# A gated linear-attention block: k's rope by plain transfers and one more VectorE operation

## The chip, the cores and the metric

The kernel is one launch on one core of one Trainium2 chip. The metric is the device time in microseconds (us). Everything is in float32; the large matrix products are made of three products of parts (high by high, low by high, high by low), which is why each weight and each activation exists as a `_hi` and a `_lo` tile.

## The reference, cut to what matters

The block takes x (2048 tokens of 512), normalises it, and computes an attention part and a feed-forward part that gates it. The attention part has 16 heads of 128 channels. For q and k of each head:

```python
q = causal_dwconv(silu(x @ Wq), conv_q_w)      # 4 taps; k and v alike
def rot_half(u):
    u1, u2 = jnp.split(u, 2, axis=-1)
    return jnp.concatenate([-u2, u1], axis=-1)
q = q * cos + rot_half(q) * sin
k = k * cos + rot_half(k) * sin
q = q / max(norm(q), 1e-12); k = k / max(norm(k), 1e-12)
for s in range(4):                             # the 4 lags
    attn = (q * lag(k, s)).sum(-1) / sqrt(128)
    out += attn * sigmoid(lag(a, s) * b) * lag(v, s)
out = out * rsqrt(mean(out * out) + eps) * norm_w * silu(x @ Wz)
s = out @ Wout
```

The result is x + s * silu(ffn(x)). The two lines of the rope are what the change is about. On the chip the 128 channels of a head lie on the 128 partitions, so rot_half moves data from partitions 0 to 63 to partitions 64 to 127 and back. [...]

## The kernel before, in words

The attention part is a software pipeline over 64 steps: head h = 0 to 15, and in each head four chunks g = 0 to 3 of 512 tokens. A step is counted c = 4h + g. Each of the five engines has a `step` function with its own order of the work, in which `c - 1`, `c - 2` and so on are chunks of earlier steps. There is no scheduler: the order is the order of the code, and the engines meet at counting semaphores.

- **TensorE** (`step`, L1070) projects q, k and v of chunk c (12 products each, L997), turns the squares for the norms (L1054), projects z of chunk c-2, computes the scores of chunk c-2 (L1066) and the sums over the values of chunk c-3 (L1042).
- **ScalarE** reads the projections out through silu (L662), makes the first tap of each convolution (L676) and the squares (L703, L704).
- **VectorE** (`step`, L880) does the other nine taps (`conv_tap`, L812), transposes v (`turn_v`, L852), does its part of the rope (`rope`, L831 and L835), reduces the norms (`sum_fold`, L842), multiplies the scores by the gates and by a band mask (`gate_scores` L858, `mask_band` L867), joins and scales the output (L818, `make_o` L875), and in g = 3 splits the next head's weights of q, k and v (`split_lo`, L823), in g = 1 those of z. TensorE's first product for a head's k waits for `wlo_k` (`wait(pe, wlo_done[n], h + 1)`, L994).
- **GpSimd (POOL)** (`step`, L577) starts the accumulating transfers (`fold_squares` L568, `add_swapped` L574, `add_squares` L562), takes the roots of the norms (`roots`, L528 and L532), and makes the gates (`make_gates`, L548 to L556).
- **SyncE (SP)** (`step`, L437) issues the plain transfers, in this order in a step: weights, `store_v` of c-1 (L416), `store_rq` of c (three small stores of the roots, L402 to L405), `load_rq` of c-2 (L412), `store_o` (L430), `load_v` of c-1 (four, L426). `load_rq` waits until the three stores have landed (L409), and `make_gates` for chunk c-2 waits for `load_rq` in the next step.

The rope of n in "qk" before: VectorE writes `rot = y * cos` (L831) and `swapped = y * sin` (L835, with the sign in the table), then POOL's `add_swapped` starts two transfers of 64 partitions each that add `swapped` to `rot` with the halves exchanged (L573 to L575). The scores wait for those transfers through `wait_rope` (L332, L1059 to L1062). For k, the two VectorE operations stand in the step after the one that made y_k: `rope("k", 0, ...)` after the first q tap and `rope("k", 1, ...)` after the second.

After the 64 steps the last chunks run out of the pipeline, and the feed-forward and the output product follow, which the change does not touch.

Of the kernel before, what the change touches and what calls it, by code (L numbers as in the profile page):

```python
# [205 lines left out]
def attention(nc, env):  # L206
# [20 lines left out]
    NC = H * G  # L227
    HALF = D // 2
# [69 lines left out]
    conv_done = {n: sem(f"conv_done_{n}") for n in "qkv"}  # L298
    rope_done = {n: sem(f"rope_done_{n}") for n in "qk"}
    rope_asked = sem("rope_asked")  # L300
    rope_added = {n: [sem(f"rope_added_{n}{i}") for i in range(2)] for n in "qk"}
    squares_done = sem("squares_done")
    fold_asked = sem("fold_asked")
    folded = sem("folded")
# [26 lines left out]

    def wait_rope(eng, n, g, c):  # L332

        wait(eng, rope_added[n][g % 2], 32 * (c // 2 + 1) if isinstance(c, int) else
             c * 16 + (32 if g % 2 == 0 else 16))

    def wait_v(eng, g, c):
# [30 lines left out]
    def cols(g):  # L368
        return slice(g * CH, (g + 1) * CH)

    def on_sync(sp):
# [65 lines left out]
        def step(h, g):  # L437
            c = h * G + g
            if not is_last(h):
                if g == 0:  # L440
                    for n in "qkv":
                        load_weights(n, h + 1)
                if g == 2:
                    load_weights("z", h + 1)
            if at := back(h, g, 1):
                store_v(at[1], c - 1)
                store_rq(at[1], c)
            if at := back(h, g, 2):
                load_rq(at[1], c)
            if at := back(h, g, 3):  # L450
                store_o(at[0], at[1], c - 3)
            if at := back(h, g, 1):
                load_v(at[1], c - 1)
# [20 lines left out]
    def on_gpsimd(pool):  # L474
# [102 lines left out]
        def step(h, g):  # L577
            c = h * G + g
            if at := back(h, g, 1):
                fold_squares(at[1], c)  # L580
                add_swapped("q", at[1], c - 1)
            if at := back(h, g, 3):
                make_gates(at[1], c - 3)
            if at := back(h, g, 1):
                add_swapped("k", at[1], c - 1)
            if at := back(h, g, 4):
                add_squares(at[1], c - 4)
            if at := back(h, g, 1):
                roots(at[0], at[1], c)
                if is_start(h, g - 1):  # L590
                    pool.wait_ge(gate_done, 2)
                gate_keys(at[0], at[1], c)

        schedule(pool, step)
        for n in "qk":
            add_swapped(n, G - 1, NC - 1)
        roots(H - 1, G - 1, NC)
        gate_keys(H - 1, G - 1, NC)
        make_gates(G - 3, NC - 3)
# [7 lines left out]
    def on_scalar(act):  # L607
# [51 lines left out]
        def silu_and_tap(n, bank, h, g, c):  # L659
            wait(act, proj_done[n], c + 1)  # L660
            wait(act, conv_done[n], DVE_TAPS[n] * (c - 1))
            nc.scalar.activation(u[n][:, g % 2, HALO:], bank[:, :], ACT.Silu).then_inc(silu_done[n], 1)  # L662

            wait(act, conv_done[n], DVE_TAPS[n] * c)
            wait(act, silu_done[n], 2 * c + 1)
            if n == "v":
                wait(act, v_stored, 16 * (c - 1))
            else:
                wait(act, rope_done[n], 2 * (c - 1))
            if g < G - 1:  # L670
                nc.scalar.activation(u[n][:, (g + 1) % 2, 0:HALO], bank[:, CH - HALO:CH], ACT.Silu
                                     ).then_inc(silu_done[n], 1)
            else:
                nc.scalar.activation(u[n][:, 0, 0:HALO], rot["q"][:, S:S + HALO], ACT.Copy
                                     ).then_inc(silu_done[n], 1)
            nc.scalar.activation(y[n][:, g % 2, :], u[n][:, g % 2, 0:CH], ACT.Copy,  # L676
                                 scale=cw[n][:, bass.ds(h * TAPS, 1)]).then_inc(tap_done[n], 1)
# [70 lines left out]
        square_out(NC - 4)  # L748
        silu_z(G - 2, NC - 2, bank_kz)
        for n in "qk":  # L750
            act.wait_ge(rope_done[n], 2 * NC)
            for i in range(2):
                act.wait_ge(rope_added[n][i], 16 * NC)
        ffn.hidden(0, 0)
        save_spill(G - 3, NC)
        silu_z(G - 1, NC - 1, bank_qv)
# [14 lines left out]
    def on_vector(dve):  # L771
# [53 lines left out]

        def rope(n, i, g, c):

            wait(dve, conv_done[n], 3 * c + 3)
            if i == 0:
                wait(dve, scores_done, c - 3)  # L830
                op = nc.vector.tensor_tensor(rot[n][:, cols(g)], y[n][:, g % 2, :], cos[:, cols(g)], ALU.mult)  # L831
            else:
                if not (isinstance(c, int) and c < 2):
                    wait_rope(dve, n, g, c - 2)
                op = nc.vector.tensor_tensor(swapped[n][:, g % 2, :], y[n][:, g % 2, :], sin[:, cols(g)],  # L835
                                             ALU.mult)
            op.then_inc(rope_done[n], 1)
# [42 lines left out]
        def step(h, g):  # L880
# [14 lines left out]
            if at3:  # L895
                gate_scores(at3[1], c - 3)
                mask_band(at3[1], c - 3)
            conv_tap("k", 3, h, g, c)
            if is_start(h, g):
                dve.wait_ge(ab_turned, 1)  # L900
# [47 lines left out]
        turn_v(G - 1, NC - 1)  # L948
        rope("k", 0, G - 1, NC - 1)
        rope("k", 1, G - 1, NC - 1)  # L950
        sum_fold(G - 1, NC)
        gate_scores(G - 3, NC - 3)
        mask_band(G - 3, NC - 3)
# [15 lines left out]
    def on_tensor(pe):  # L969
# [86 lines left out]

        def score(g2, k):
            ahead = 1 if g2 < G - 1 else 0
            wait_rope(pe, "k", g2, k)  # L1059
            wait_rope(pe, "q", g2, k)  # L1060
            if ahead:
                wait_rope(pe, "q", g2 + 1, k + 1)  # L1062
# [543 lines left out]
```

## Time and profile before

| | |
|---|---|
| median of 3 runs | 1326.75 us (1324.55 to 1327.91) |
| profiled execution | 1327.47 us, of which 1325.7 us span from the first to the last instruction |
| TensorE busy (matmul) | 1292.8 us, 98% of the span |
| VectorE busy | 954.7 us, 72% |
| ScalarE busy | 720.5 us, 54% |
| GpSimd busy | 641.8 us, 48% |
| attention steps, by the slices of the page | about 70 to 890 us |

The busy shares are means over stages with different limits: VectorE is at 9 tenths and more in the attention steps and at 2 to 4 tenths behind them. A matmul's end is modelled, so a TensorE that reads 98% may still have been held up by short waits; the rows below are read for those. The granted TensorE clock is at 9 tenths or more of full speed in all but one of the 40 slices of the page.

### The profile page before, as it was taken

How to read it: one execution, taken by the hardware profiler on the slowest of the kernel's cores; microseconds unless marked ns; L12 is line 12 of the kernel's file. 1: busy time of each engine (PE TensorE's matmuls, PEld its weight loads, DVE VectorE, ACT ScalarE, POOL GpSimd, SP SyncE). 2: the span in 40 equal slices, each digit the busy share in tenths (PEclk: the TensorE clock that was granted, in tenths of full speed). 3: DMA queues.
4: the chain of work that ended last, by engine and by line, in shares of the span. 5: the costliest groups of instructions: out<-in, count | busy, mean ns of one | idle time of the engine just before them, and what ended most of it. 6: DMA issues, size and time to landing. Idle time of an engine off the chain costs nothing.

```text
span 1325.7 us, 22085 instructions
## 1 busy us (share of the span) xinstructions
PE 1292.8 (98%) x6312; PEld 1078.7 (81%) x6312; DVE 954.7 (72%) x1530; ACT 720.5 (54%) x1377; POOL 641.8 (48%) x827
## 2 busy tenths in 40 slices
PE   6989999999999999999999999998999999999998
PEld 5778888888888888888888888877888888888886
DVE  7879999989999999899999998993122322423442
ACT  5656666666666666666666666664543444422221
POOL 6357676777776767767767777763000000000001
PEclk9989999999999999999999999999999999999999
DMA  8258888888797888787878787868510101246544
GB/s 267 63 108 174 157 157 157 169 149 171 139 177 149 163 155 166 153 170 142 174 153 162 150 164 154 153 121 221 178 47 18 47 16 56 85 154 213 184 124 138
DMA packets 276875, 188.89 MB, mean 142 GB/s; under 512 B 167904, under 2 KB 204768, under 8 KB 276576
## 3 DMA queue, kind: packets, MB, share of 16 engines
q1 hardware_dynamic: 238064, 121.48, 34.1%
q0 software_dynamic: 38768, 66.87, 31.1%
q8 instruction: 23, 0.38, 0.1%
q14 instruction: 20, 0.16, 0.1%
HBM read 79.36 MB, written 42.08 MB: 92 GB/s over the span
## 4 chain that ended last, share of the span: by engine, by line
PE 77%; DVE 11%; issue 5%; DMA 3%; POOL 2%; ACT 2%; SPq 1%; DVEq 0%; POOLq 0%; ACTq 0%
PE bank L997 37%; PE bank L1491 13%; PE bank L1294 9%; PE bank L1281 8%; PE bank L1066 3%; PE bank L1042 3%; DVE y_k L812 2%; DVE y_q L812 2%; PE bank L1054 2%; DVE y_v L812 2%; PE bank L987 1%; ACT y_q L676 1%; DMA rq_win<-rq_scratch 1%; DVE coef L858 1%; DVE rot_k L831 1%
## 5 line engine op out<-in xcount | busy, mean ns | idle before, releaser
L812 DVE SCALAR_TENSOR_TENSOR y_q<-u_q,cw_q,y_q 128x512 f32<-128x512 f32 x192 | 143.0, 745 | 57.7 <-ACT y_q L676 57.6
L1362 POOL TENSOR_TENSOR g_buf<-g_buf,up_raw 128x512 f32<-128x512 f32 x3 | 3.8, 1280 | 356.2 <-DVE g_buf L1422 356.2
L1270 DVE TENSOR_TENSOR hid_lo<-relu,hid_hi 128x512 fp32r<-128x512 f32 x64 | 44.3, 693 | 166.4 <-ACT hid_hi L1262 166.4
L812 DVE SCALAR_TENSOR_TENSOR y_k<-u_k,cw_k,y_k 128x512 f32<-128x512 f32 x192 | 143.4, 747 | 1.3 <-ACT y_k L676 1.1
L812 DVE SCALAR_TENSOR_TENSOR y_v<-u_v,cw_v,y_v 128x512 f32<-128x512 f32 x192 | 143.4, 747 | 0.6
L532 POOL TENSOR_TENSOR rnorm<-norms,neg_half 128x8 f32<-128x8 f32 x64 | 125.0, 1953 | 9.6 <-POOL norms L528 8.6
L574 POOL DMA_DIRECT2D rot_q<-swapped_q x128 | 107.5, 996 | 43.4 <-DVE swapped_q L835 24.1
L574 POOL DMA_DIRECT2D rot_k<-swapped_k x128 | 107.3, 977 | 38.9 <-issue 25.3
L1258 ACT ACTIVATE relu<-bank,us_sb 128x512 f32<-128x512 f32 x64 | 44.1, 690 | 126.3 <-PE bank L1281 119.2
L568 POOL DMA_DIRECT2D down_raw<-down_raw x63 | 59.2, 940 | 91.0 <-ACT down_raw L704 81.4
L1382 ACT ACTIVATE hid_hi<-o_raw 128x512 fp32r<-128x512 f32 x64 | 40.2, 630 | 115.9 <-PE bank L1491 95.2
L1442 DVE TENSOR_TENSOR hid_lo<-o_raw,hid_hi 128x512 fp32r<-128x512 f32 x64 | 43.8, 690 | 79.9 <-ACT hid_hi L1382 79.9
L1491 PE MATMUL bank<-x_hi,hid_hi 128*128 128x512 f32 x256 | 99.6, 389 | 0.0
L1491 PE MATMUL bank<-x_hi,hid_lo 128*128 128x512 f32 x256 | 99.6, 389 | 0.0
L1491 PE MATMUL bank<-x_lo,hid_hi 128*128 128x512 f32 x256 | 99.6, 389 | 0.0
L528 POOL TENSOR_SCALAR norms<-norms 128x8 f32<-128x8 f32 x64 | 97.2, 1518 | 4.9 <-DVE norms L842 4.9
L562 POOL DMA_DIRECT2D sq_sum<-out_sq x62 | 90.9, 1467 | 2.5 <-issue 2.5
L662 ACT ACTIVATE u_v<-bank 128x512 f32<-128x512 f32 x64 | 38.4, 600 | 71.0 <-PE bank L997 71.0
L1066 PEld LDWEIGHTS bank<-rot_q,rot_k 128*128 128x128 f32 x512 | 68.1, 191 | 10.3 <-issue 5.5
L997 PE MATMUL bank<-x_hi,whi_z 128*128 128x512 f32 x256 | 75.6, 417 | 0.0
L1294 PE MATMUL bank<-down_sign_b,hid_hi 128*128 128x512 f32 x192 | 74.8, 390 | 0.4 <-DVE hid_lo L1270 0.4
L1294 PE MATMUL bank<-down_sign_b,hid_lo 128*128 128x512 f32 x192 | 74.7, 389 | 0.0
(189 smaller groups left out, 3514.8 us busy)
## 6 DMA issues: line engine op xcount, KB each, us to landing
rot_q<-swapped_q POOLq DMA_DIRECT2D x128, 128.0 KB, 4.5
v_scratch<-y_v SPq DMA_DIRECT2D x64, 256.0 KB, 3.6
rot_k<-swapped_k POOLq DMA_DIRECT2D x128, 128.0 KB, 4.1
v_tok<-v_scratch SPq DMA_DIRECT2D x256, 64.0 KB, 3.8
o_scratch<-o_buf SPq DMA_DIRECT2D x64, 256.0 KB, 3.5
o_raw<-o_scratch SPq DMA_DIRECT2D x64, 256.0 KB, 4.2
down_raw<-down_raw POOLq DMA_DIRECT2D x63, 256.0 KB, 3.4
sq_sum<-out_sq POOLq DMA_DIRECT2D x62, 256.0 KB, 5.4
```

Of the source, the lines that this page charges most:

```text
L528: nc.gpsimd.tensor_scalar(norms[:, g1 % 2, :], norms[:, g1 % 2, :], NORM_FLOOR, None, ALU.max).then_inc(floor_done, 1)
L532: nc.gpsimd.tensor_tensor(rnorm[:, g1 % 2, :], norms[:, g1 % 2, :], neg_half[:, 0:2 * BC], ALU.pow).then_inc(root_done, 1)
L562: nc.gpsimd.dma_start(sq_sum[:, cols(g)], squares, accum_op=ALU.add).then_inc(sq_added, 16)
L568: nc.gpsimd.dma_start(fold[g1 % 2], other[g1 % 2], accum_op=ALU.add).then_inc(folded, 16)
L574: nc.gpsimd.dma_start(rot[n][to:to + HALF, cols(g1)], swapped[n][frm:frm + HALF, g1 % 2, :], accum_op=ALU.add).then_inc(rope_added[n][g1 % ...
L812: nc.vector.scalar_tensor_tensor(y[n][:, g % 2, :], u[n][:, g % 2, i:i + CH], cw[n][:, bass.ds(h * TAPS + i, 1)], y[n][:, g % 2, :], ALU.m ...
L997: last = nc.tensor.matmul(bank[:, :], w[n][:, i % KT, :], part[:, i % KT, cols(g)], start=(i == 0), stop=(i == TERMS - 1))
L1066: last = nc.tensor.matmul(scores[:, b, :], rot["k"][:, at:at + P], rot["q"][:, at:at + BW], start=True, stop=True)
L1270: nc.vector.tensor_tensor(hid_lo[:, j % HS, :], relu[:, j % 2, :], hid_hi[:, j % HS, :].bitcast(fp32), ALU.subtract).then_inc(hid_lo_done, 1)
L1281: last = nc.tensor.matmul(up_bank(n, j), up_group(j // WG)[:, t, j % WG * P:(j % WG + 1) * P], part[:, t, bass.ds(n * CH, CH)], start=(k = ...
L1294: last = nc.tensor.matmul(acc_of(n)[b], part[:, j % HS, b * P:(b + 1) * P], down_group(j // WG)[:, j % WG, :], start=(j == 0 and part is h ...
L1491: last = nc.tensor.matmul(sums[b], part[:, h % HS, b * P:(b + 1) * P], wo_tile(w, h // KT, h % KT), start=(h == 0 and k == 0), stop=(h == ...
```

## The change

k's rope is done in another way; q's stays. SP's `step` gets two plain transfers that copy y_k with its halves exchanged into `swapped_k`, issued once the third k tap of the same chunk is done. They stand ahead of `store_v`, so everything that SP issues later in the step stands behind that wait. VectorE, in the next step, multiplies `swapped_k` by the sines in place (where it made `swapped_k` from y_k before) and, further down, subtracts it from `rot_k`: a third operation, `rope("k", 2, ...)`, between `mask_band` and the third k tap. POOL's `add_swapped("k", ...)` goes, with its two accumulating transfers a step. The scores wait for VectorE's subtraction instead of for the transfers.

```diff
+    swap_in = [sem(f"swap_in{i}") for i in range(2)]
+    ROPE_OPS = {"q": 2, "k": 3}
@@ wait_rope
-        wait(eng, rope_added[n][g % 2], 32 * (c // 2 + 1) if isinstance(c, int) else
+        landed = rope_added["q"] if n == "q" else swap_in
+        wait(eng, landed[g % 2], 32 * (c // 2 + 1) if isinstance(c, int) else
@@ SP step, between load_weights and store_v
+            wait(sp, conv_done["k"], 3 * c + 3)
+            wait(sp, rope_done["k"], 3 * (c - 1))
+            for to, frm in ((0, HALF), (HALF, 0)):
+                sp.dma_start(swapped["k"][to:to + HALF, g % 2, :], y["k"][frm:frm + HALF, g % 2, :]
+                             ).then_inc(swap_in[g % 2], 16)
@@ POOL step
-            if at := back(h, g, 1):
-                add_swapped("k", at[1], c - 1)
@@ POOL, behind the steps
-        for n in "qk":
-            add_swapped(n, G - 1, NC - 1)
+        add_swapped("q", G - 1, NC - 1)
@@ VectorE rope
+            elif n == "k" and i == 1:
+                wait_rope(dve, n, g, c)
+                sw = swapped["k"][:, g % 2, :]
+                op = nc.vector.tensor_tensor(sw, sw, sin[:, cols(g)], ALU.mult)
+            elif n == "k":
+                wait(dve, rope_done[n], 3 * c + 2)
+                op = nc.vector.tensor_tensor(rot[n][:, cols(g)], rot[n][:, cols(g)], swapped["k"][:, g % 2, :],
+                                             ALU.subtract)
@@ VectorE step, behind mask_band
+            if at1:
+                rope("k", 2, at1[1], c - 1)
             conv_tap("k", 3, h, g, c)
@@ TensorE score
-            wait_rope(pe, "k", g2, k)
+            wait(pe, rope_done["k"], 3 * (k + 1))
```

VectorE in a g = 3 step, from the second k tap to the split of the next head's wk, before:

```order
L812 SCALAR_TENSOR_TENSOR y_k<-u_k,cw_k,y_k 128x512 [waits conv_done_k]
L858 TENSOR_TENSOR coef<-bank,gates 128x528 [waits gates_done,scores_done]
L867 TENSOR_TENSOR coef<-coef,const 128x528 [waits gated]
L812 SCALAR_TENSOR_TENSOR y_k<-u_k,cw_k,y_k 128x512 [waits conv_done_k]
L823 TENSOR_TENSOR wlo_q<-raw_q,whi_q 128x512 [waits whi_done_q]
L812 SCALAR_TENSOR_TENSOR y_v<-u_v,cw_v,y_v 128x512 [waits tap_done_v]
L831 TENSOR_TENSOR rot_q<-y_q,cos 128x512 [waits conv_done_q]
L812 SCALAR_TENSOR_TENSOR y_v<-u_v,cw_v,y_v 128x512 [waits conv_done_v]
L818 TENSOR_TENSOR bank<-bank,carry 128x2x4 [waits spill_saved]
L812 SCALAR_TENSOR_TENSOR y_v<-u_v,cw_v,y_v 128x512 [waits conv_done_v]
L823 TENSOR_TENSOR wlo_k<-raw_k,whi_k 128x512 [waits whi_done_k]
```

The same stretch in the changed kernel, whose lines are numbered anew:

```order
L817 SCALAR_TENSOR_TENSOR y_k<-u_k,cw_k,y_k 128x512 [waits conv_done_k]
L872 TENSOR_TENSOR coef<-bank,gates 128x528 [waits gates_done,scores_done]
L881 TENSOR_TENSOR coef<-coef,const 128x528 [waits gated]
L844 TENSOR_TENSOR rot_k<-rot_k,swapped_k 128x512 [waits rope_done_k]
L817 SCALAR_TENSOR_TENSOR y_k<-u_k,cw_k,y_k 128x512 [waits conv_done_k]
L828 TENSOR_TENSOR wlo_q<-raw_q,whi_q 128x512 [waits whi_done_q]
L817 SCALAR_TENSOR_TENSOR y_v<-u_v,cw_v,y_v 128x512 [waits tap_done_v]
L837 TENSOR_TENSOR rot_q<-y_q,cos 128x512 [waits conv_done_q]
L817 SCALAR_TENSOR_TENSOR y_v<-u_v,cw_v,y_v 128x512 [waits conv_done_v]
L823 TENSOR_TENSOR bank<-bank,carry 128x2x4 [waits spill_saved]
L817 SCALAR_TENSOR_TENSOR y_v<-u_v,cw_v,y_v 128x512 [waits conv_done_v]
L828 TENSOR_TENSOR wlo_k<-raw_k,whi_k 128x512 [waits whi_done_k]
```

The subtraction (L844) stands ahead of the third k tap and of the two splits that TensorE's next head begins with.

SP in one step (g = 3 in the first head), before:

```order
L416 DMA v_scratch<-y_v 128x512 [waits v_turned]
L402 DMA rq_scratch<-rnorm 128x4 [waits root_done]
L403 DMA rq_scratch<-rnorm 4x3
L405 DMA rq_scratch<-rnorm 4x1
L412 DMA rq_win<-rq_scratch 128x1x32 [waits rq_stored]
L430 DMA o_scratch<-o_buf 128x512 [waits o_done]
L426 DMA v_tok<-v_scratch 32x16x32 [waits v_stored]
L426 DMA v_tok<-v_scratch 32x16x32 x3
```

SP in the same step of the changed kernel:

```order
L451 DMA swapped_k<-y_k 64x512 [waits rope_done_k,conv_done_k]
L451 DMA swapped_k<-y_k 64x512
L419 DMA v_scratch<-y_v 128x512 [waits v_turned]
L405 DMA rq_scratch<-rnorm 128x4 [waits root_done]
L406 DMA rq_scratch<-rnorm 4x3
L408 DMA rq_scratch<-rnorm 4x1
L415 DMA rq_win<-rq_scratch 128x1x32 [waits rq_stored]
L433 DMA o_scratch<-o_buf 128x512 [waits o_done]
L429 DMA v_tok<-v_scratch 32x16x32 [waits v_stored]
L429 DMA v_tok<-v_scratch 32x16x32 x3
```

The store of y_v and the three stores of the roots are now issued behind a wait for VectorE's third k tap and behind two transfers of 128 KB.

POOL in one step, before, from the gates to the roots:

```order
L556 TENSOR_TENSOR gates<-rq_own,gate_k 128x16 [waits gated,rnorm_done,rq_joined]
L574 DMA rot_k<-swapped_k 64x512 [waits rope_done_k]
L574 DMA rot_k<-swapped_k 64x512
L562 DMA sq_sum<-out_sq 128x512 [waits out_sq_done]
L528 TENSOR_SCALAR norms<-norms 128x8 [waits norms_done]
L532 TENSOR_TENSOR rnorm<-norms,neg_half 128x8 [waits rq_stored,floor_done]
```

In the changed kernel the two middle transfers are gone and the rest keeps its order.

## Rows read from the trace of the kernel before

**Rows 1.** Who waited for whom, TensorE: us in total, times, longest
```profile
PE bank L997 <- DVE wlo_k L823: 3.9, 15, 0.3
```

**Rows 2.** Timeline of VectorE, 335 to 376 us: start, us, instruction, idle before
```profile
335.50 0.75 DVE L812 SCALAR_TENSOR_TENSOR y_q<-u_q,cw_q,y_q 128x512 f32<-128x512 f32 x1 [0.75 <-ACT y_q L676]
...
341.24 0.69 DVE L858 TENSOR_TENSOR coef<-bank,gates 128x528 f32<-128x528 f32 x1
...
342.59 0.74 DVE L812 SCALAR_TENSOR_TENSOR y_k<-u_k,cw_k,y_k 128x512 f32<-128x512 f32 x1
...
348.71 0.75 DVE L812 SCALAR_TENSOR_TENSOR y_q<-u_q,cw_q,y_q 128x512 f32<-128x512 f32 x1 [1.40 <-ACT y_q L676]
...
351.24 0.71 DVE L835 TENSOR_TENSOR swapped_k<-y_k,sin 128x512 f32<-128x512 f32 x1
...
356.47 0.69 DVE L823 TENSOR_TENSOR wlo_q<-raw_q,whi_q 128x512 fp32r<-128x512 f32 x1
357.09 0.74 DVE L812 SCALAR_TENSOR_TENSOR y_v<-u_v,cw_v,y_v 128x512 f32<-128x512 f32 x1
...
359.80 0.69 DVE L823 TENSOR_TENSOR wlo_k<-raw_k,whi_k 128x512 fp32r<-128x512 f32 x1
...
375.58 0.75 DVE L812 SCALAR_TENSOR_TENSOR y_q<-u_q,cw_q,y_q 128x512 f32<-128x512 f32 x1 [1.22 <-ACT y_q L676]
```

**Rows 3.** Timeline of TensorE, the same columns
```profile
343.38 1.06 PE L1042 MATMUL bank<-coef,v_tok 128*128 128x132 f32 x8
344.20 1.17 PE L997 MATMUL bank<-x_hi,whi_q 128*128 128x512 f32 x4
...
357.38 1.17 PE L997 MATMUL bank<-x_hi,whi_q 128*128 128x512 f32 x4
...
360.63 1.17 PE L997 MATMUL bank<-x_hi,whi_k 128*128 128x512 f32 x4 [0.26 <-DVE wlo_k L823]
...
371.10 1.17 PE L997 MATMUL bank<-x_hi,whi_q 128*128 128x512 f32 x4
```

**Rows 4.** Timeline of SP's queue: when each transfer is issued
```profile
338.41 0.61 SPq L435 DMA_DIRECT2D raw_z<-in_wz  x1
339.14 0.70 SPq L416 DMA_DIRECT2D v_scratch<-y_v  x1
...
346.30 0.29 SPq L405 DMA_DIRECT2D rq_scratch<-rnorm  x1
347.47 0.57 SPq L412 DMA_DIRECT2D rq_win<-rq_scratch  x1
...
371.98 0.28 SPq L405 DMA_DIRECT2D rq_scratch<-rnorm  x1
375.01 0.59 SPq L412 DMA_DIRECT2D rq_win<-rq_scratch  x1
```

**Rows 5.** Lines L416 (all, then the one at 367.3) and L412: issue ns, landing us
```profile
L416 SPq DMA_DIRECT2D v_scratch<-y_v x64: 339/610/1944, 52.6 to 900.3; - x64
DMA to landing us min/median/max: 2.1/3.6/7.0
...
L416 SPq DMA_DIRECT2D v_scratch<-y_v x1: 476/476/476, 367.3 to 367.3; - x1
DMA to landing us min/median/max: 7.0/7.0/7.0
...
DMA to landing us min/median/max: 2.0/3.1/5.1
```

**Rows 6.** Timeline of POOL, the same columns as for VectorE
```profile
350.29 0.48 POOL L548 TENSOR_TENSOR rq_win<-rq_win,const 128x32 f32<-128x32 f32 x1 [0.73 <-DMA rq_win<-rq_scratch]
...
351.48 0.55 POOL L556 TENSOR_TENSOR gates<-rq_own,gate_k 128x16 f32<-128x16 f32 x1
```

**Rows 7.** The costliest groups on VectorE: busy us, mean ns
```profile
L835 DVE TENSOR_TENSOR swapped_k<-y_k,sin 128x512 f32<-128x512 f32 x64 | 45.0, 704 | 0.0
...
L835 DVE TENSOR_TENSOR swapped_q<-y_q,sin 128x512 f32<-128x512 f32 x64 | 43.6, 681 | 0.0
```

More of the change, by code:

```diff
@@ L300, in attention @@
     rope_asked = sem("rope_asked")
-    rope_added = {n: [sem(f"rope_added_{n}{i}") for i in range(2)] for n in "qk"}
+    rope_added = {"q": [sem(f"rope_added_q{i}") for i in range(2)]}
+    swap_in = [sem(f"swap_in{i}") for i in range(2)]
+    ROPE_OPS = {"q": 2, "k": 3}
     squares_done = sem("squares_done")
@@ L668, in silu_and_tap @@
             else:
-                wait(act, rope_done[n], 2 * (c - 1))
+                wait(act, rope_done[n], ROPE_OPS[n] * (c - 1))
             if g < G - 1:
@@ L750, in on_scalar @@
         for n in "qk":
-            act.wait_ge(rope_done[n], 2 * NC)
-            for i in range(2):
-                act.wait_ge(rope_added[n][i], 16 * NC)
+            act.wait_ge(rope_done[n], ROPE_OPS[n] * NC)
+        for i in range(2):
+            act.wait_ge(rope_added["q"][i], 16 * NC)
         ffn.hidden(0, 0)
@@ L826, in rope @@
         def rope(n, i, g, c):
-            wait(dve, conv_done[n], 3 * c + 3)
+            if n == "q" or i == 0:
+                wait(dve, conv_done[n], 3 * c + 3)
             if i == 0:
@@ L950, in on_vector @@
         rope("k", 1, G - 1, NC - 1)
+        rope("k", 2, G - 1, NC - 1)
         sum_fold(G - 1, NC)
```

## The prediction, made before the changed kernel was run

> **What bounds the kernel now.** I read the list of waits of TensorE and VectorE first, then one head of each engine's timeline, then the transfers. The reader is to see three things.
>
> First, TensorE sets the pace of the attention steps. Its products for q start at 344.20 and 357.38 us, so a step takes 13.18 us; the next start is at 371.10, so the step that begins at 357.38 takes 13.72 [rows 3]. The difference, 0.54 us, is its wait for `wlo_k`, of which 0.26 shows as idle time. That wait comes in 15 places, once for each head but the last, 3.9 us in all [rows 1]. A head is thus 3 x 13.18 + 13.72 = 53.26 us.
>
> Second, VectorE is nearly full. In three steps of four it runs through its list and then waits for the first q tap: 0.75 us in front of 335.50, 1.40 in front of 348.71, 1.22 in front of 375.58 [rows 2]. In the g = 3 step, with three splits of weights, it has no idle time from 348.71 on. There the whole list up to the split at 359.80 is a chain, and TensorE's k products start when it ends, 360.49 against 360.63 [rows 2, 3]. So an operation more in an ordinary step is free, and in a g = 3 step, ahead of `wlo_k`, it is paid in full.
>
> Third, a loop runs beside these: roots (POOL), three small stores, `load_rq` (SP), gates (POOL), roots. POOL waits 0.73 us for `rq_win` at 350.29 [rows 6]. The gates end at 351.48 + 0.55 = 352.03. `gate_scores` stands 5.74 us behind the first q tap (341.24 - 335.50), so it is due at 348.71 + 5.74 = 354.45 [rows 2]. The gates are early by 2.42 us. The change hangs SP on this path.
>
> **The change, part by part.** The profiled execution took 1327.47 us, 1.8 more than its span and 0.7 above the median of the runs; I sum against the median, 1326.75.
>
> *The subtraction.* A VectorE operation of this shape costs its successor 0.62 us, from the start of `wlo_q` at 356.47 to the next tap at 357.09 [rows 2]; I take 0.61. Bounds: its busy time, 0.70, from above [rows 7]; nothing from below, if its slot were idle, as in three steps of four. There the idle time of 0.75, 1.40 and 1.22 becomes 0.14, 0.79 and 0.61, so it stays hidden, and VectorE still meets the g = 3 step on time. With that cover gone it would cost 0.61 in all 64 steps, 39 us. In the 15 g = 3 steps: 15 x 0.61 = 9.2 us. TensorE's q products of the new head wait too (`wlo_q` ends at 357.16, they start at 357.38), but that is the same 0.61, not a second one. The new head is 53.87 us, 13.47 a step.
>
> *The multiplication* keeps its place and its time, now waiting for the swap. The swap is issued when the third k tap ends (343.33, later by 0.61 with the subtraction ahead), the second half about 0.7 later. A landing like that of `v_scratch`, 3.6 [rows 5], gives 348.2; the multiplication of the next step is at 351.24 [rows 2]. 3 us are left. In g = 0, with three loads of weights ahead in the queue, 7.0 [rows 5] would leave -0.4, which the 0.61 idle of that step takes. Cost: 0, at most 2 in all.
>
> *POOL's two issues of k* go, and with them the time between the gates and the roots. The roots come earlier, but SP is then behind its own wait, so no gain while the steps run. In the last three steps, which run out of the pipeline, an earlier root could help by up to 1 us each, my estimate; bounds -3 and 0, and I take 0.
>
> *What SP holds back.* SP waits 8.4 us into the step (third k tap of 335.50 ends at 343.33, plus 0.61) and then issues swap, swap, `store_v`, three root stores, `load_rq`, `store_o`, four `load_v`. `store_v` was issued at 339.14, 3.6 us into the step, now at about 9.9. ScalarE writes that buffer of y_v again two steps after it was filled, late in the next step: hidden. `load_v` is wanted two steps later: hidden. The weights are wanted three steps later: hidden. What isn't clearly hidden is `load_rq`, since it closes a new loop: `gate_scores` of a chunk, mask, subtraction, third k tap, SP's swaps, `store_v`, root stores, `load_rq`, gates, `gate_scores` of the next chunk. Its length:
> - `gate_scores` start to the end of the third k tap: 343.33 - 341.24 = 2.09 [rows 2], with the subtraction 2.70;
> - two issues of SP at 0.61 [rows 5] and gaps: 1.4;
> - landing of `store_v`: 3.6, the median, and about that with the 256 KB of `raw_z` issued just ahead at 338.41 [rows 4, 5]; ends taken at 2.8 and 4.6, inside the row's 2.1 and 7.0 (the 7.0 has three loads of 256 KB ahead, where the new order has one such amount);
> - from there to `load_rq`: in [rows 4, 5] the store issued at 367.3 lands at 374.4, and `load_rq`, which waits only for the root stores issued by 371.98, goes at 375.01: 0.6. With nothing ahead they need 347.47 - 346.30 = 1.17 [rows 4];
> - landing of `load_rq`: 3.1, from 2.0 to 5.1 [rows 5];
> - POOL, 350.29 to 352.03, and hand-overs: 1.8 [rows 6].
>
> That is 2.70 + 1.4 + 3.6 + 0.6 + 3.1 + 1.8 = 13.2 us, against 13.47 a step. With the low ends (2.8, 2.0) it is 11.3; with 4.6 and 3.6 for the landings, 14.7. The gates are then early not by 2.4 but by some 0.3, and TensorE has some 0.7 more: the mask ends about where the third k tap starts, 342.59, and the products that read it start at 343.38 [rows 2, 3]. I take it that the loop just fits on average and that late landings cost now and then: 3 us over the 60 steps. Low end 0; high end 60 x (14.7 - 13.47) = 74.
>
> The root stores' delay is what the row at 371.98 shows: 3.0 us instead of 1.17, ending with `store_v`. The Trainium skill (DMA: Bandwidth & Descriptors, section "Queues, rings and completion order") says why: a completion increment is strongly ordered and lands only after every earlier write of that DMA engine, across its queues. By that rule the loop is the 13.2 us above in every step; without it, the stores would need their 1.17 from about 2 us behind the swaps, the loop would be near 11.6, and the sum would be 1326.75 + 9.2. The trace agrees with the rule at that row.
>
> Sum: 1326.75 + 9.2 + 3 = 1339 us.
>
> **The rivals.**
>
> *The SP loop sets the pace.* For it: two transfers and a store stand ahead of the root stores in every step, and with each term a little over its median it passes 13.47. Against it: the lowest landing of `store_v` is 2.1 [rows 5], and POOL's accumulating transfers of k, which shared the DMA engines, are gone. At 13.8 us a step the 60 steps take 60 x 13.8 = 828 instead of 15 x 53.26 = 799: +29, 1356 us. It decides above a mean loop of 13.47, and each 0.1 more is 6 us.
>
> *Not slower: VectorE gets its 0.61 back.* POOL's k transfers are issued beside VectorE's work. `swapped_k`, which runs near them, takes 704 ns, `swapped_q` 681 [rows 7]. If POOL's quiet gives each of the some 20 operations ahead of `wlo_k` 0.03 us, the subtraction is paid, and with the 3 us of late landings kept and the 3 us of the last steps won the time is 1327, between 1323 and 1330. It decides from 0.03 us an operation. Against it: 0.023 us is the mean difference of those two groups over all 64 steps, they share one form, and only a few of the 20 run beside POOL's k transfers.
>
> *The swap comes late.* VectorE stalls at the multiplication. It needs a landing of over 6.5 us outside of g = 0; at a stall of 0.5 in the 15 g = 3 steps, 8 us more: 1347.
>
> *The change doesn't do what it says* can't well be: the instructions of the changed program show the swaps and the third operation.
>
> **How the numbers follow.** Forecast (the subtraction in 15 steps, the loop just hidden): 0.50, its own range 1333 to 1346. SP's loop: 0.32, 1346 to about 1400. Not slower: 0.12. Late swap: 0.06. The range leaves out the upper part of the loop's case (0.08) and most of the third case: 1329 to 1366. A difference of 0.3%, 4 us, is about what a measurement can tell: faster than 1322.8 has 0.05, within 0.3% 0.09, slower 0.86.
>
> **What would show it.** Right: TensorE's wait for `wlo_k` or `wlo_q` in 15 places grows by 0.61, a head takes 53.9 us, and VectorE's wait for ScalarE's q tap shrinks by 0.6 in the other steps. `load_rq` is issued some 14 us into a step where it was 12. Wrong: VectorE waits for the gates (L858 of before) in most steps, or TensorE for `coef`, and a step is longer than 13.2 in g = 0, 1 and 2. It is wrong as well if VectorE waits at the in-place multiplication, or if a head still takes 53.3 us.

## The result, and the profile after

| | before | after |
|---|---|---|
| median | 1327.42 us (1324.55 to 1329.59, 9 runs) | 1333.35 us (1330.58 to 1335.40, 9 runs) |
| ratio, after to before | | 1.0045, 95% interval 1.0032 to 1.0058 |
| span of the profiled execution | 1325.7 us | 1330.0 us |
| VectorE busy | 954.7 us | 992.5 us |
| GpSimd busy | 641.8 us | 525.2 us |

The changed kernel is slower by 0.45%, about 6 us. The forecast was 1339 with a range of 1329 to 1366. A second set of runs of the changed kernel gave the same (the first experiment below).

I cut both traces at three places: the start of the first full step (the products with `whi_q` at 77.81 us before, 75.78 after), the start of those products sixty steps later (876.62 and 883.75), and the first matmul of the feed-forward's second product (the `down` product, L1294 before, at 916.28 and 921.44). In us:

| stretch | before | after | difference |
|---|---|---|---|
| start, to the first full step | 77.81 | 75.78 | -2.03 |
| sixty steps (15 heads) | 798.81 | 807.96 | +9.15 |
| last four steps, out of the pipeline | 39.66 | 37.70 | -1.96 |
| from the feed-forward's second product to the end of the span | 409.38 | 408.56 | -0.82 |
| span | 1325.65 | 1330.01 | +4.36 |

The steps lose 9.15, which is 15 x 0.61, and the three other stretches give back 4.8. The reading goes in that order.

**The steps.** VectorE's timeline in the changed kernel, from the end of a g = 2 step to the start of the g = 1 step of the next head (start us, us, instruction, idle before):
```profile
349.65 0.75 DVE L817 SCALAR_TENSOR_TENSOR y_q<-u_q,cw_q,y_q 128x512 f32<-128x512 f32 x1 [0.80 <-ACT y_q L681]
...
352.18 0.71 DVE L841 TENSOR_TENSOR swapped_k<-swapped_k,sin 128x512 f32<-128x512 f32 x1
...
355.40 0.70 DVE L872 TENSOR_TENSOR coef<-bank,gates 128x528 f32<-128x528 f32 x1
...
356.75 0.68 DVE L844 TENSOR_TENSOR rot_k<-rot_k,swapped_k 128x512 f32<-128x512 f32 x1
357.36 0.74 DVE L817 SCALAR_TENSOR_TENSOR y_k<-u_k,cw_k,y_k 128x512 f32<-128x512 f32 x1
358.02 0.70 DVE L828 TENSOR_TENSOR wlo_q<-raw_q,whi_q 128x512 fp32r<-128x512 f32 x1
...
361.35 0.68 DVE L828 TENSOR_TENSOR wlo_k<-raw_k,whi_k 128x512 fp32r<-128x512 f32 x1
...
377.13 0.75 DVE L817 SCALAR_TENSOR_TENSOR y_q<-u_q,cw_q,y_q 128x512 f32<-128x512 f32 x1 [0.62 <-ACT y_q L681]
```
Against [rows 2]: the subtraction (L844) takes its place between the mask and the third k tap, and the tap follows it after 357.36 - 356.75 = 0.61. The idle time ahead of the first q tap is 0.80 where it was 1.40, and 0.62 where it was 1.22. Over all its waits VectorE's idle time for that tap went from 57.6 to 28.5 us (below). In the g = 3 step there is none to take from, and `wlo_k` comes 0.61 later behind the first q tap: 361.35 - 349.65 = 11.70 where [rows 2] have 359.80 - 348.71 = 11.09.

TensorE's timeline at the same place:
```profile
345.13 1.17 PE L1014 MATMUL bank<-x_hi,whi_q 128*128 128x512 f32 x4
...
358.77 1.20 PE L1014 MATMUL bank<-x_hi,whi_q 128*128 128x512 f32 x4 [0.21 <-DVE wlo_q L828]
...
362.18 1.17 PE L1014 MATMUL bank<-x_hi,whi_k 128*128 128x512 f32 x4 [0.39 <-DVE wlo_k L828]
...
372.64 1.17 PE L1014 MATMUL bank<-x_hi,whi_q 128*128 128x512 f32 x4
```
The two steps around the new head take 358.77 - 345.13 = 13.64 and 372.64 - 358.77 = 13.87, where [rows 3] have 13.18 and 13.72: 0.46 of the new wait sits at `wlo_q` and the remaining 0.15 at `wlo_k`. The list of waits shows both (us in total, times, longest):
```profile
PE bank L1014 <- DVE wlo_k L828: 5.6, 15, 0.4
PE bank L1014 <- DVE wlo_q L828: 3.3, 15, 0.3
...
DVE y_q L817 <- ACT y_q L681: 28.5, 43, 2.8
...
DVE coef L872 <- POOL gates L564: 5.7, 2, 3.4
```
The idle time in this list is 5.6 + 3.3 against 3.9 in [rows 1], 5.0 more, while the starts of the products are 9.15 later. Idle time is counted from a modelled end of the matmul before, so the starts are the better ruler. The wait of VectorE for the gates has only 2 places, both in the last four steps. So neither SP's loop nor the multiplication holds VectorE.

**SP's queue**, the same stretch of the changed kernel:
```profile
344.91 1.15 SPq L451 DMA_DIRECT2D swapped_k<-y_k  x2
346.11 0.58 SPq L419 DMA_DIRECT2D v_scratch<-y_v  x1
346.73 0.45 SPq L405 DMA_DIRECT2D rq_scratch<-rnorm  x1
...
347.63 0.29 SPq L408 DMA_DIRECT2D rq_scratch<-rnorm  x1
349.01 0.59 SPq L415 DMA_DIRECT2D rq_win<-rq_scratch  x1
```
and the landings of L451 (swap), L419 (`store_v`) and L415 (`load_rq`), us:
```profile
L451 SPq DMA_DIRECT2D swapped_k<-y_k x128: 461/581/1230, 46.1 to 897.3; - x128
...
DMA to landing us min/median/max: 2.2/2.4/3.1
```
```profile
DMA to landing us min/median/max: 2.5/2.7/3.8
```
```profile
L415 SPq DMA_DIRECT2D rq_win<-rq_scratch x64: 557/591/605, 78.7 to 912.8; - x64
...
DMA to landing us min/median/max: 2.0/2.1/4.6
```
Everything that I had priced from [rows 5] lands sooner: the swap in 2.4 (3.6 taken), `store_v` in 2.7 (3.6), `load_rq` in 2.1 (3.1). The gates then come:
```profile
351.21 0.49 POOL L556 TENSOR_TENSOR rq_win<-rq_win,const 128x32 f32<-128x32 f32 x1
351.78 0.56 POOL L559 TENSOR_TENSOR rq_own<-rq_win 128x16 f32<-128x16 f32 x1
352.42 0.56 POOL L564 TENSOR_TENSOR gates<-rq_own,gate_k 128x16 f32<-128x16 f32 x1
```
They end at 352.98 and `gate_scores` starts at 355.40: early by 2.42, as in [rows 2, 6]. The median over the steps is 2.42 in both kernels, the lower quarter 1.09 after.

**The DMA engines.** The profile's queue rows, before and after (queue, packets, MB, share of 16 engines' span):
```profile
q1 hardware_dynamic: 238064, 121.48, 34.1%
q0 software_dynamic: 38768, 66.87, 31.1%
```
```profile
q1 hardware_dynamic: 248304, 138.27, 39.3%
q0 software_dynamic: 28528, 50.09, 23.4%
```
The 16.8 MB of k's halves took 31.1 - 23.4 = 7.7 points as accumulating transfers of GpSimd and 39.3 - 34.1 = 5.2 as plain ones of SyncE.

### The profile page after: what moved, and what is told of

It reads as the page before. It is cut to its first block, busy times and chain, and to the rows that moved or that the text cites. A ratio compares the mean times of both kernels' runs of the same rounds, so it can differ in the third digit from the quotient of the medians.

```text
span 1330.0 us, 22162 instructions
## 1 busy us (share of the span) xinstructions
PE 1295.7 (97%) x6312; PEld 1079.0 (81%) x6312; DVE 992.5 (75%) x1594; ACT 720.3 (54%) x1377; POOL 525.2 (39%) x699
## 3 DMA queue, kind: packets, MB, share of 16 engines
q1 hardware_dynamic: 248304, 138.27, 39.3%
q0 software_dynamic: 28528, 50.09, 23.4%
## 4 chain that ended last, share of the span: by engine, by line
PE 78%; DVE 12%; issue 4%; ACT 2%; DMA 1%; POOL 1%; SPq 1%; DVEq 0%; POOLq 0%; ACTq 0%
PE bank L1014 39%; PE bank L1508 13%; PE bank L1311 9%; PE bank L1298 8%; PE bank L1083 3%; PE bank L1059 3%; DVE y_k L817 2%; DVE y_q L817 2%; PE bank L1071 2%; DVE y_v L817 2%; PE bank L1004 1%; DVE coef L872 1%; ACT y_q L681 1%; DVE rot_k L844 1%; DVE wlo_k L828 1%
## 5 line engine op out<-in xcount | busy, mean ns | idle before, releaser
L817 DVE SCALAR_TENSOR_TENSOR y_q<-u_q,cw_q,y_q 128x512 f32<-128x512 f32 x192 | 143.0, 745 | 29.1 <-ACT y_q L681 28.5
L540 POOL TENSOR_TENSOR rnorm<-norms,neg_half 128x8 f32<-128x8 f32 x64 | 108.3, 1692 | 9.6 <-POOL norms L536 8.6
L1014 PE MATMUL bank<-x_hi,whi_q 128*128 128x512 f32 x252 | 74.2, 416 | 3.9 <-DVE wlo_q L828 3.3
L1014 PE MATMUL bank<-x_hi,whi_k 128*128 128x512 f32 x256 | 70.4, 397 | 5.6 <-DVE wlo_k L828 5.6
L1014 PE MATMUL bank<-x_hi,whi_z 128*128 128x512 f32 x256 | 75.5, 417 | 0.0
L667 ACT ACTIVATE u_q<-bank 128x512 f32<-128x512 f32 x64 | 38.4, 600 | 67.2 <-PE bank L1014 67.2
```

What stands on the lines that cost most here:

```text
L540: nc.gpsimd.tensor_tensor(rnorm[:, g1 % 2, :], norms[:, g1 % 2, :], neg_half[:, 0:2 * BC], ALU.pow).then_inc(root_done, 1)
L817: nc.vector.scalar_tensor_tensor(y[n][:, g % 2, :], u[n][:, g % 2, i:i + CH], cw[n][:, bass.ds(h * TAPS + i, 1)], y[n][:, g % 2, :], ALU.m ...
L1014: last = nc.tensor.matmul(bank[:, :], w[n][:, i % KT, :], part[:, i % KT, cols(g)], start=(i == 0), stop=(i == TERMS - 1))
```

## The experiments

Each is measured against the kernel before on the same chip. "Head" is four steps of TensorE: the sum of the medians of the steps g = 0, 1, 2 and 3 over the heads.

**The changed kernel again.**

> The changed kernel as it is, beside its variants on the same chip. Theory: 1333 us; four steps of a head take 53.88 us, the kernel before 53.26; VectorE's subtraction is paid in the 15 g = 3 steps (15 x 0.61 = 9.2 us), and some 3 us come back at the start and the end of the 64 steps. Rival (the last is chance of one execution): the start and the end differ from run to run by as much, and the next profile shows other numbers there.

Measured: 1332.27 us against 1325.49, ratio 1.0049 (1.0035 to 1.0063), head 53.85. The loss stands, and the theory with it: this second profile cuts into 75.71, 808.02, 38.12 and 408.52 us, within 0.1 us of the first at the start, in the steps and at the end, and 0.42 off in the last four steps.

**The subtraction at the end of VectorE's step**, where the idle time is.
```
-            if at1:
-                rope("k", 2, at1[1], c - 1)
             conv_tap("k", 3, h, g, c)
...
                 split_lo("v", h + 1)
+            if at1:
+                rope("k", 2, at1[1], c - 1)
```


> The subtraction of k's rope moved to the end of VectorE's step, behind the split of wv, so that it no longer stands ahead of wlo_q and wlo_k. Theory (the cost is the subtraction's place in the g = 3 step): a head takes 53.26 us again, and the time falls by 15 x 0.61 = 9.2 us, to 1324. Rival (the cost is SP's held back loads or the transfers themselves): a head stays at 53.88, 1333 us. Rival (VectorE is so full that the place doesn't matter): the wait for coef or the next head's wait takes it back, 1330 to 1333.

Measured: 1327.26 us, ratio 1.0011 (1.0002 to 1.0020), span 1323.8. The head falls from 53.86 to 53.42, not to 53.25. `wlo_q` no longer appears and `wlo_k` is back at 3.9 us in 15 places, so the 0.61 ahead of it is gone:
```profile
PE bank L1014 <- DVE wlo_k L828: 3.9, 15, 0.3
```
What is left is in the g = 0 step. The subtraction now stands behind `wlo_v` in the g = 3 step, and as that step has no idle time, it shifts the next one: `gate_scores` ends late and the scores start at 369.15, not 13.18 but 13.79 behind those at 355.36:
```profile
355.36 1.06 PE L1083 MATMUL bank<-rot_q,rot_k 128*128 128x132 f32 x8
...
369.15 1.15 PE L1083 MATMUL bank<-rot_q,rot_k 128*128 128x132 f32 x8
```
So moving it took away 0.44 of the 0.61; 0.17 comes back as a wait for the gated scores.

**The subtraction left out** (k's rope then lacks its second half; the transfers, the waits and the multiplication stay).
```
-            if at1:
-                rope("k", 2, at1[1], c - 1)
...
-            op.then_inc(rope_done[n], 1)
+            op.then_inc(rope_done[n], 2 if n == "k" and i == 1 else 1)
```


> Leaves the subtraction out (the scores read k times cosine only); all transfers and waits stay. Theory: 53.26 us a head and 1324 us, the same as with the subtraction moved to the end of the step, and this kernel shows what the rest of the change is worth by itself: some 3 to 4 us less than the kernel before, from the start and the end of the steps. Rival (SP's swaps and their wait cost as well): not below the kernel before, 1327 or more.

Measured: 1323.47 us, ratio 0.9985 (0.9976 to 0.9994), head 53.25, as before the change. The subtraction alone carries the loss in the steps, and the rest of the change is a small gain of 2 us.

**One more VectorE operation of the same shape**, ahead of the subtraction (a maximum of `swapped_k` with itself).
```
+                nc.vector.tensor_tensor(sw, sw, sw, ALU.max).then_inc(extra_done, 1)
+                wait(dve, extra_done, c + 1)
```


> One more VectorE operation of the same shape ahead of the subtraction in every step (a maximum of swapped_k with itself, which changes no value). Theory (an operation is free while VectorE has idle time in the step, and paid in full in g = 3): the idle time left in a head is some 1.5 us, four more operations are 2.4 to 2.9 us, so VectorE now sets the pace: a head takes 53.88 + 0.9 to 1.4 us, the time rises by 14 to 20 us over the changed kernel, to 1347 to 1353. Rival (only the g = 3 steps pay): 15 x 0.61 = 9 us, 1342. Rival (every operation is paid): 64 x 0.61 = 39 us, 1372.

Measured: 1353.14 us, ratio 1.0208 (1.0191 to 1.0226), head 54.90. It costs 1.04 a head, more than its slot of 0.61, and the time is at the upper edge of what the theory allowed. Against the changed kernel on the same chip (1332.27) it is 21 us: the sixty steps take 824.24 where they took 808.02, and the rest is at the start (78.33) and in the last four steps (39.63). Idle time ahead of the q products of the new head:
```profile
368.03 1.21 PE L1018 MATMUL bank<-x_hi,whi_q 128*128 128x512 f32 x4 [1.04 <-DVE wlo_q L829]
...
371.44 1.17 PE L1018 MATMUL bank<-x_hi,whi_k 128*128 128x512 f32 x4 [0.35 <-DVE wlo_k L829]
```
The second operation eats the cover that was left in the other steps too, so VectorE no longer meets the g = 3 step on time. The price of an operation is not linear.

**`store_v` ahead of the swaps** in SP's queue.
```
+            if at := back(h, g, 1):
+                store_v(at[1], c - 1)
             wait(sp, conv_done["k"], 3 * c + 3)
...
             if at := back(h, g, 1):
-                store_v(at[1], c - 1)
                 store_rq(at[1], c)
```


> SP issues the store of y_v ahead of the two swaps instead of behind them, 6 us earlier in the step. The root stores then have only the swaps ahead of them. Theory (SP's loop is hidden by 1 to 2.4 us): load_rq goes 0.3 to 1 us earlier in most steps, and the time stays at 1333. Rival (the loop costs some us with late landings): 2 to 4 us faster than the changed kernel.

Measured: 1333.36 us, ratio 1.0056 (1.0043 to 1.0070), head 53.86. SP's queue has `store_v` 4.5 us ahead of the swaps, the root stores no longer wait for it, and POOL's wait for `rq_win` falls to 8.4 us in 14 places, from 40.1 in 34 and 28.1 in 24 in the two profiles of the changed kernel:
```profile
342.26 0.61 SPq L419 DMA_DIRECT2D v_scratch<-y_v  x1
346.74 1.15 SPq L453 DMA_DIRECT2D swapped_k<-y_k  x2
347.95 0.58 SPq L405 DMA_DIRECT2D rq_scratch<-rnorm  x1
...
350.15 0.59 SPq L415 DMA_DIRECT2D rq_win<-rq_scratch  x1
```
```profile
  POOL rq_win L557: 8.4, 14
```
Not a microsecond comes of it: the sixty steps take 808.04. Relief on SP's loop is worth nothing, so the loop was not the bound. That is the direct evidence against the first rival. One more row of this kernel is needed below. With k's accumulating transfers gone but `store_v` back at its old place in the step, 3.7 us behind the first q tap, it lands no sooner than before (3.6), but later (line L419, all 64):
```profile
DMA to landing us min/median/max: 2.7/4.3/5.8
```

**GpSimd issues the plain swaps**, at the end of its step, in place of SP.
```
-            wait(sp, conv_done["k"], 3 * c + 3) ... the two swaps, in SP's step
...
                 gate_keys(at[0], at[1], c)
+            wait(pool, conv_done["k"], 3 * c + 3) ... the two swaps, in GpSimd's step
```

> The swaps are issued by POOL at the end of its step instead of by SP; they stay plain transfers. SP's order and POOL's number of transfers are then those of the kernel before. Theory (the 3 to 4 us at the start and the end come from POOL and the DMA engines having less to do): heads stay at 53.88 us; POOL's two issues are back but stand behind the roots, so most of the gain stays, 1332 to 1335. Rival (SP's hold on store_v and the roots costs something in the steps): faster than the changed kernel by over 2 us.

Measured: 1335.10 us, ratio 1.0074 (1.0061 to 1.0087). The head is 53.85 again; the first full step starts at 79.83 instead of 75.78, since the swaps now stand ahead of the first fold, for which TensorE waits 6.0 us at the start. Who issues the swaps makes no difference to the steps.

**The kernel before with the two weight splits earlier**: `wlo_q` ahead of the third k tap, `wlo_k` ahead of the second v tap.
```
+            if g == 3 and not is_last(h):
+                split_lo("q", h + 1)
             conv_tap("k", 3, h, g, c)
...
+            if g == 3 and not is_last(h):
+                split_lo("k", h + 1)
             conv_tap("v", 2, h, g, c)
```


> The kernel before, with VectorE's splits of wq and wk for the next head moved up in the g = 3 step: wq's ahead of the third k tap, wk's ahead of the second v tap. Theory (TensorE loses 0.54 us a head to wlo_k, only because of the order): a head takes 52.72 us, 15 x 0.54 = 8 us less, 1319. Rival (TensorE then waits for coef in g = 0, since VectorE begins that step as late as before): half of it or less, 1323 to 1327.

Measured: 1319.41 us, ratio 0.9956 (0.9943 to 0.9970), head 52.81. The waits for `wlo_k` are gone from the list. The chain ahead of the splits was the bound of the kernel before; that the same chain carries the changed kernel's loss is what the two experiments on the subtraction show.

**Both**: early splits, the subtraction last, and in the g = 0 step the gates' multiplication and the mask ahead of `sum_fold` and the second k tap.
```
+            if at3 and g == 0:
+                gate_scores(at3[1], c - 3)
+                mask_band(at3[1], c - 3)
             if at1:
                 sum_fold(at1[1], c)
             conv_tap("k", 2, h, g, c)
-            if at3:
+            if at3 and g > 0:
```


> The changed kernel with the subtraction at the end of the step, the splits of wq and wk moved up as in the other kernel of this set, and in g = 0 the gates and the mask ahead of the sum of the norms and the second k tap. Theory: VectorE's work of a head is some 52.3 us and TensorE's 52.72, so TensorE has no wait left: 52.72 us a head, 1.16 less than the changed kernel, 15 x 1.16 = 17 us: 1316. Rival (VectorE at 99% passes its late times on to TensorE through coef or the q tap): 1319 to 1325.

Measured: 1318.60 us, ratio 0.9947 (0.9934 to 0.9961), head 52.91. It beats both kernels, and misses its own forecast by 2.6. The gain over the early splits alone is not separated: the intervals overlap.

**The same in the g = 1 step as well** (`g < 2` in place of `g == 0`).

> The version with the subtraction at the end of VectorE's step and the two weight splits early, and with the gates' multiplication and the mask ahead of sum_fold and k's third tap in the stages g = 1 as well as g = 0. Theory: the 0.16 us a head that g = 1 is over 13.18 us is TensorE's scores waiting for the gated keys; with the gates ahead there too the head goes from 52.91 to about 52.75 us, and the time from 1318.6 to about 1316. Rival: in g = 1 the gates' multiplication is not what is late; the head stays at 52.9 and the time at 1318 to 1319.

Measured: 1321.21 us, ratio 0.9946 (0.9933 to 0.9960), span 1320.1 against 1318.1, head 53.08. A miss: no gain. The g = 1 step is at 13.18 as expected, but the g = 2 step, which was at 13.19, now takes 13.52, and up to the last steps VectorE waits for the gates in 13 places, 11 of them in g = 1 steps, where it did in one:
```profile
DVE coef L872 <- POOL gates L564: 4.3, 13, 0.8
```
Against the version before it:
```profile
DVE coef L872 <- POOL gates L564: 1.1, 1, 1.1
```
VectorE has no idle time ahead of its first q tap in the steps g = 0, 1 and 2, so a wait for the gates in g = 1, like this one,
```profile
380.06 0.71 DVE L872 TENSOR_TENSOR coef<-bank,gates 128x528 f32<-128x528 f32 x1 [0.51 <-POOL gates L564]
```
makes the unmoved multiplication of the next step (394.48) late by as much, and TensorE's scores wait for that one:
```profile
395.32 1.14 PE L1086 MATMUL bank<-rot_q,rot_k 128*128 128x132 f32 x8 [0.47 <-DVE coef L872]
```
The g = 2 step follows the wait ahead of it: 13.2 to 13.3 us in the four heads without one, 13.5 to 13.6 behind a wait of 0.22 (the first and the last head aside), 13.9 behind 0.51 and 14.3 behind 0.84. The wait moved; it did not go.

**The kernel before without k's accumulating transfers** (k's swapped half is not added, and nothing waits for it).
```
-            if at := back(h, g, 1):
-                add_swapped("k", at[1], c - 1)
...
-            wait_rope(pe, "k", g2, k)
+            wait(pe, rope_done["k"], 2 * (k + 1))
```


> The kernel before, with GpSimd's accumulating transfers for k left out and nothing put in their place: k's rope is incomplete (the swapped half is not added), and nothing waits for it. VectorE, TensorE and ScalarE do the same instructions as before, so the steps stay at 53.25 us a head. Theory: what the change gives back (about 5 us of the 9.15 that the subtractions cost) comes from these transfers being gone, whatever takes their place: the start 1.5 to 2 us earlier, the end 0.9 us shorter (GpSimd's final drain 1.9 us in place of 3.9), the tail perhaps 0 to 2 us; about 1323 us where the kernel before has 1325 to 1327, a ratio near 0.997 to 0.998. Rival: the three differences come from somewhere else (SyncE's queue, the order of issues in the tail), and this one stays at the kernel before's time, its drain at 3.9 us.

Measured: 1324.35 us, ratio 0.9967 (0.9953 to 0.9982), head 53.27. The first full step starts at 76.62 (-1.2), the last four steps take 40.27 (+0.6), the rest 408.51 (-0.9). The end's gain belongs to these transfers: every kernel without them has 408.5 there, the two with them 409.4. The last four steps' gain does not. At the start 1.2 of the 2.0 us came with them in this profile, but that is not settled: the kernels that lack them start their first full step anywhere from 75.5 to 79.8. The theory holds for the end, the rival for the last steps.

This kernel too is needed below for the landing of `store_v`, which stands in its old place and has less traffic beside it (its line L416, all 64):
```profile
DMA to landing us min/median/max: 2.8/4.5/6.8
```

## Why the prediction was right, point by point

**What bounds the kernel: right.** A head of 53.26 was read and 53.25 measured; 53.87 was forecast and 53.86 measured. The early splits, which touch only that chain, give 5.6 us (1319.41 against 1325.04 on their chip; 15 x 0.44 by the heads is 6.6), which confirms the bound by removing it.

**The subtraction: right, 9.2 forecast and 9.15 measured**, at the place named and with the idle times named (0.79 and 0.61 forecast, 0.80 and 0.62 measured). Without it the head is 53.25 again. "TensorE's q products of the new head wait too" was right as well: most of the 0.61 shows there.

**The multiplication at 0: right.** It runs in 702 ns a piece, without idle time in front. The swap lands 2.4 us after its issue, 3.1 at the most, so the cover is 4 us and more.

**SP's loop, 3 us taken and up to 74 kept in the range: the term that was mis-sized.** It costs nothing. Its 13.2 us were made of landings measured at the old places in the step: 3.6 and 3.1 became 2.7 and 2.1, and the swap's issue needs 0.58. With these the loop is 2.70 + 1.2 + 2.7 + 0.4 + 2.1 + 1.8 = 10.9 us against 13.47. I had named the quieter DMA engines as an argument against that rival. The runs don't bear that out as the reason: where `store_v` keeps its old place and k's accumulating transfers are gone, it lands in 4.3 us (plain swaps behind it) and in 4.5 (no swaps at all), not in less than 3.6. What is left is the new place: before, it was issued right behind four `load_v` and, in two steps of four, weights (at 339.14 behind the 338.41 of [rows 4]); after, SP has issued nothing for 3.9 us when the swaps of 344.91 go, and only they stand ahead of it. The root stores do wait for `store_v`: the third, issued at 347.63, lets `load_rq` go at 349.01, which is 0.4 behind the landing of `store_v` (348.61); in 53 of the 64 steps it goes 0.19 to 0.57 us behind that landing. By the rule in the Trainium skill (DMA: Bandwidth & Descriptors, section "Queues, rings and completion order"), a completion lands only after the earlier writes of its DMA engine; the row agrees. The 0.6 that I took for this was right; it simply had room. The loop "near 11.6" that I gave for the case without the rule does not follow from its own parts (2.70 + 1.4 + 2 + 1.17 + 3.1 + 1.8 = 12.2); the forecast did not use it.

The landing of `load_rq` depends on its place as well. In the kernel before, GpSimd's fold and `load_rq` stand close together:
```profile
346.61 0.94 POOL L568 DMA_DIRECT2D down_raw<-down_raw  x1 [0.48 <-issue]
```
The fold lands at 350.04 and `load_rq`, issued at 347.47 [rows 4], at 350.21. In 47 of the 64 steps before, its landing is 0.17 to 0.25 us behind that of a fold; after the change in 12. Its median landing falls with the distance at which it is issued behind the fold: 3.1 us at a median of 0.5 (before), 2.7 at 1.1 (the subtraction left out), 2.1 at 1.9 (the changed kernel), and 2.1 at 11.8 (k's transfers left out). The second and third have the same transfers, so it is not their number. A landing of 3.1 in [rows 5] was thus largely somebody else's transfer, and the row should have been read with the queue of the other engine beside it.

**POOL's k issues at 0, bounds -3 to 0: the place was too narrow.** I looked for a gain in the last steps alone. The start (-2.0) was not in the sum. There TensorE waits for the first fold, ahead of which no k transfer stands, but beside which two are in flight in the kernel before:
```profile
68.91 1.64 POOL L574 DMA_DIRECT2D rot_k<-swapped_k  x2 [0.39 <-issue]
```
```profile
71.32 1.08 PE L1054 MATMUL bank<-const,down_raw 128*128 128x128 f32 x4 [4.18 <-DMA down_raw<-down_raw]
...
73.91 1.91 PE L997 MATMUL bank<-x_hi,wlo_z 128*128 128x512 f32 x4
```
and after:
```profile
70.47 1.08 PE L1071 MATMUL bank<-const,down_raw 128*128 128x128 f32 x4 [2.93 <-DMA down_raw<-down_raw]
...
73.06 1.15 PE L1014 MATMUL bank<-x_hi,wlo_z 128*128 128x512 f32 x4
```
The fold lands 0.85 us earlier. Leaving the k transfers out gave a wait of 3.8 and 1.2 of the 2.0 us. For the remaining 0.8 a `store_v` that is issued beside the fold before (66.52) and not after (61.58) suggests itself, but in the kernel with the subtraction last it is away from the fold as well (60.95), and there the fold takes 4.8 us to land, in the changed kernel 4.0. The load of `raw_z` fits better: the fold takes 4.0 us in the three profiles in which it is issued 0.6 us ahead of that load (the changed kernel twice, the subtraction left out), and 4.8 to 5.3 in seven others, where it goes with that load or behind it. The kernel with one more operation (0.6 ahead, 4.95) does not fit, so this stays open. From there on the clock adds to it: TensorE, idle for 4.2 us in the one and 2.9 in the other, comes back at a granted clock of 0.50 (1.2 GHz) in both, and from 73 to 77 us has 0.55 in the one (full speed, 2.4 GHz, from 76.56 on) and 0.98 in the other (from 73.17 on), so that the same four products take 1.91 and 1.15.

The last four steps gave 1.96, inside the bounds, but not for the reason given: both without the transfers (40.27) and with the swaps but no subtraction (39.66) there is no gain, while most kernels with both have 36.7 to 38.1 and the one with an extra operation has 39.6. VectorE's waits for the gates (L858 before, L872 after) in these steps go with it: 8.4 to 9.6 us in all in the four kernels without the gain (39.7 to 40.3), 5.1 to 6.6 in the seven with it, 6.7 in the one with an extra operation. Why the gates come late in the one and not in the other was not tested and stays open.

**The rivals.** SP's loop: refuted by the early gates and by `store_v` first. VectorE gets its 0.61 back: refuted. `swapped_k` takes 702 ns where it took 704, and `swapped_q` 682 for 681; VectorE is no faster for GpSimd's quiet. That the time came near the upper end of that rival's range (1333.35 against 1330) is due to the start and the end, not to VectorE. Late swap: refuted, no wait at L841.

The sum with measured terms: +9.15 (subtraction), 0 (loop), -2.03 (start), -1.96 (last steps), -0.82 (end) = +4.3 in the profiled pair; the medians differ by 5.9. The forecast of +12 was 6 too high: 3 for the loop, and 3 for the gains at the start, in the last steps and at the end (4.8 in the profiled pair). The measured 1333.35 lies at the very edge of the forecast's own range (1333 to 1346). The place and the size of the main cost were read rightly; the total was twice what was measured. That the time still fell inside is in part luck: both misses went the same way, and half a microsecond more of gain at the start or the end would have put it below that range.

**One sign did not come.** `load_rq` was to be issued some 14 us into a step; it goes 12.6 us in (349.01, first q tap at 336.43), where it was 12.0. That is the mis-sized loop again.

## What to carry to other kernels

An operation more on an engine with idle time in three steps of four is paid in the fourth, at its spacing in the timeline (0.61 here, not its busy time of 0.70), and the way out is to put it, or what stands ahead of the last product, on the other side of the instruction that is waited for: moving two splits gave about 6 us, as much as the whole change cost. When a change moves a transfer to another place in the step, its landing must be priced for that place, by what is in flight beside it there (`store_v`: 3.6 at the old, 2.7 at the new), and a landing that ends just behind another engine's transfer is not the transfer's own. Pulling one wait forward pays only until the next one stands there, as the gates did when the g = 1 step was changed too.

## What the runs showed of the hardware that I had not expected

**The end of the program is longer with k's accumulating transfers.** GpSimd's last additions start at 1317.72, 1322.99 and 1317.33 us before, after, and in the kernel before without k's transfers:
```profile
1317.72 3.77 POOL L1362 TENSOR_TENSOR g_buf<-g_buf,up_raw 128x512 f32<-128x512 f32 x3 [356.24 <-DVE g_buf L1422]
```
```profile
1322.99 3.77 POOL L1379 TENSOR_TENSOR g_buf<-g_buf,up_raw 128x512 f32<-128x512 f32 x3 [356.30 <-DVE g_buf L1439]
```
```profile
1317.33 3.77 POOL L1359 TENSOR_TENSOR g_buf<-g_buf,up_raw 128x512 f32<-128x512 f32 x3 [356.24 <-DVE g_buf L1419]
```
From their end to the end of the span (1325.7, 1330.0, 1324.4) it is 4.2, 3.2 and 3.3 us. GpSimd's records close with a drain that ends 3.93 us after its last operation in the first and 1.89 in the two others. The kernel in which GpSimd issues plain swaps, with as many transfers as before (383), has 1.93: it is the accumulating kind for k that goes with the long drain, not the number of transfers. Why was not tried.

**Accumulating transfers cost the DMA engines more for the same bytes**: 7.7 points against 5.2, as above. These 16.8 MB changed queue and kind at once, but two other kernels part the two. With k's transfers left out, and with the plain swaps issued by GpSimd, GpSimd's queue has:
```profile
q0 software_dynamic: 28528, 50.09, 23.2%
```
```profile
q0 software_dynamic: 34672, 66.87, 27.5%
```
For the same bytes on the same queue that is 27.5% with plain swaps and 31.1% with accumulating ones (31.3 in the kernel before with early splits), 4.3 and 7.9 points above the row without them. That row's share is between 23.2 and 24.6 in the nine profiles that have it, so such a difference is good to some 1.4 points. The 3.6 points between the kinds are more than that: it is the accumulating kind that costs more, not the queue.
